# A hand-planned transformer kernel on one core: the first q stores move to SP's queue, the rows of maxima to ScalarE's, small loads and an all-reduce go ahead of the feed-forward loads

## The chip, the cores and the metric

One core of a Trainium2 chip. The metric is the device time of one execution in microseconds (us), the median of several runs. TensorE is called PE, VectorE DVE, ScalarE ACT, GpSimd POOL, SyncE SP. "SPq" and "ACTq" in rows of the profile are DMAs issued from SP's and ACT's sequencers.

## The reference, cut to what matters

Two layers over 8 batches of 256 tokens, 512 wide. Layer 0 is causal ALiBi attention with 32 heads of 16 and one shared key and value head, plus a top-2-of-4 LoRA mixture. Layer 1 is a 16x16 attention inside each token plus a gated feed-forward of 1792.

```python
xn = _layernorm(x)
x = x + attn0(xn, Wqkv, Wo) + lora_moe(xn, A, B, Wr)
xn = _layernorm(x)
gate, up = dequant(xn, gate_wq, gate_scale), dequant(xn, up_wq, up_scale)
x = x + attn1(xn, Wq, Wk, Wv) + dequant(silu(gate) * up, down_wq, down_scale)
```

## The kernel before, in words

The tokens are worked in 4 chunks of 512 (c = 0 to 3), each of 2 batches (i = 0 to 7). Matrix products run on fp16 pairs, high and low part, three products for one. For each batch the kernel computes q, k and v, the scores once to find row maxima (step max, L1154 on PE, L1537 on DVE), a transpose of the maxima (nmT), then the scores again with the maxima as two extra rows of q, exponentials (exp: L1176 and L1171 on PE, L998 and L999 on ACT, low halves L883 on POOL or L1549 on DVE), the product with v (pv, L1191), the output projection (L1218) and the feed-forward (gate and up L1266, down L1287).

q needs another layout than the one it is computed in. Each tile of 128 columns is stored to DRAM (q_parts) by `store_heads` (L693) in pieces of 64 bytes, 1024 pieces to a DMA, and read back as rows of the tile `qq` (gather_first L705, gather L708). For chunk 0 that is step store(b, m) on ACT's queue, two DMAs each, 16 in all. For later chunks it is step q(c, m) on SP's queue, four DMAs for each of 4 tiles. These later tiles share two buffers `qs`, so ACT's step q(c, m) waits until the tile two before it is in DRAM. The maxima go into `qq` by step nm(i), two DMAs on SP's queue (L770), and exp(i, 0, 0) on PE waits for them.

```python
n = c * NK + m
wait_full(act, "q", c, m)
if n - 2 >= NK:
    act.wait_ge(s_qd[(n - 2) % NK], 16 * 2 * NB * ((n - 2) // NK))
```

The feed-forward weights (12 loads of 448 KB, step ffn_load, L859 and L862) and nine small loads (step late, L852; late(2) alone is 1 MB) are issued from POOL, on the software DMA queue. ffn_load(0) waits for gather(1), because it overwrites the place of q's weights and of `q_first`. late(2) waits for nm(0).

The order of the steps on each engine comes from a list scheduler that runs when the file is loaded: each step has a cost (US), its predecessors with a gap (Plan.add), and a rank (RANK) that decides among steps that could start. The kernel then issues each engine's steps in that order, with semaphores. So numbers in US, in RANK and in the gaps set the order on every engine, and nothing else.

Of the kernel before, what the change touches and what calls it, by code (L numbers as in the profile page):

```python
# [109 lines left out]
RANK = {  # L110
    "PE": {"xT0": (-48.5, -1, 4), "tok": (-300.5, 0, 19, -10), "kT": (224, 0.5, -46, 146), "q0": (-50, 0.5, 13, -67),
        "norm": (-268, 3, -40, 81), "norm2": (-397.5, 0, 0, -21), "qa": (184.5, -1, 55, 284), "q": (-63, 0, 64, 3),
        "max": (-171, 0.5, -40, -10), "nmT": (-110, 2, -10, 84), "exp": (-13, 0, 0, -214), "pv": (49.5, -2, -14, -17),
        "attT": (-191, 2, 6, -16), "midT": (428.5, 0, -6, 10), "outa": (-90.5, 4, -4, -94), "out": (111.5, 3, 22, -55),
# [16 lines left out]
    "POOL": {"start": (338, 0.5, 34, 23), "ffn_load": (-280, 1, 13, 3), "ln0": (468.5, 1, -41, 144), "clear": (-81.5, 2, -1, -103),
        "turn": (176, 4, -29, 20), "norm": (-170, 1, -10, 39), "late": (244.5, 4, 0, 29), "norm2": (-191, 3, -46, 131),
        "lo": (520, -2, -13, -11), "setup1": (-258.5, 1, -53), "setup2": (491.5, 3, -40, 154), "exp": (-533, 4),
        "ln1": (-398, -2, -24, -97), "att4": (416, -2, -81, 153), "up": (-667.5, 0.5, -49, -52)},
    "SP": {"x_load": (361, 4, 3, 2), "consts": (395, -2, -26, 1), "wo": (438, 2, 247, -23), "gather_first": (-18, 3, -6, -235),
        "gather": (68, 2, -86, -160), "tables": (142, 1, -7, 41), "q": (952.5, 4, -60, 97), "nm": (211, 1, 0, 264),
        "x1_load": (-206.5, 2, -14), "down": (215.5, 2, 0, 129)},
}


# [1590 lines left out]
```

## Time and profile before

| | us |
|---|---|
| median of 3 runs | 625.62 (624.89 to 625.85) |
| the profiled execution | 625.02 |
| its span | 623.2 |
| PE busy | 570.7 (92%) |
| DVE, ACT, POOL busy | 461.3, 377.0, 351.7 |

The profiled execution's span leaves 1.8 us of its own time outside. Times of rows count from the start of the span. A row's bracket is the idle time of the engine before the row and what ended it.

### The profile page before, as it was taken

What the parts mean: (1) busy time and instruction counts of PE and PEld (TensorE: products, weight loads), DVE (VectorE), ACT (ScalarE), POOL (GpSimd) and SP (SyncE); (2) the same over time, 40 slices, a digit from 0 to 9 for tenths busy, and PEclk for the clock granted to TensorE, in tenths of its full rate; (3) what the DMA queues carried; (4) which work ended last, traced back from release to release, by engine and by line L of the source; (5) the groups of instructions that cost most, each with busy time, mean ns of one, the idle gap of its engine ahead of it and who ended that gap; (6) DMA issues with size and microseconds to landing.
All of it is one profiled execution on the core that took longest, in us unless ns stands there. A gap on an engine that the chain in (4) does not pass through costs nothing.

```text
span 623.2 us, 14286 instructions
## 1 busy us (share of the span) xinstructions
PE 570.7 (92%) x5590; PEld 421.3 (68%) x5590; DVE 461.3 (74%) x1034; ACT 377.0 (61%) x703; POOL 351.7 (56%) x364
## 2 busy tenths in 40 slices
PE   4579583699999999999999999999999999999997
PEld 4466451467885668776968587858685876785783
DVE  4769874899999874899697748996986569354642
ACT  3287095847875478675757485858684776651240
POOL 6231595724655667674837574848576677542140
PEclk9987895599999999999999999999999999999999
DMA  8767799905054146001610160016001000000000
GB/s 207 152 95 78 123 237 217 170 2 54 2 54 87 37 68 70 3 4 35 88 17 5 35 86 4 4 35 88 1 5 52 18 1 9 28 2 2 35 1 34
DMA packets 98942, 34.97 MB, mean 56 GB/s; under 512 B 75548, under 2 KB 90044, under 8 KB 98876
## 3 DMA queue, kind: packets, MB, share of 16 engines
q1 hardware_dynamic: 76044, 24.58, 22.7%
q0 software_dynamic: 2352, 7.18, 5.7%
q10 hardware_dynamic: 20480, 2.31, 2.6%
q8 instruction: 44, 0.72, 0.5%
q14 instruction: 22, 0.18, 0.1%
HBM read 30.19 MB, written 8.39 MB: 62 GB/s over the span
## 4 chain that ended last, share of the span: by engine, by line
PE 68%; DVE 13%; SPq 8%; ACT 4%; issue 3%; DMA 2%; POOL 2%; ACTq 1%; DVEq 0%
PE B_bank L1266 27%; PE B_bank L1287 14%; PE A_bank L1218 7%; SPq L693 5%; PE A_bank L1191 4%; DVE mx L1537 4%; PE A_bank L1120 3%; PE E_bank L1176 3%; PE B_bank L1154 3%; PE E_bank L1171 2%; PE B_bank L1254 1%; DMA qq<-nmp 1%; ACTq L693 1%; SPq L731 1%; SPq L717 1%
## 5 line engine op out<-in xcount | busy, mean ns | idle before, releaser
L883 POOL TENSOR_TENSOR probs<-e,probs 128x512 f16<-128x512 f32 x176 | 208.3, 1188 | 127.2 <-ACT probs L999 126.8
L1266 PE MATMUL B_bank<-xs,wgu 128*128 128x256 f16 x1792 | 204.3, 273 | 0.3 <-DVE hf L1649 0.3
L998 ACT ACTIVATE e<-E_bank,wn 128x512 f32<-128x512 f32 x192 | 133.7, 696 | 103.4 <-PE E_bank L1176 53.9
L1266 PEld LDWEIGHTS B_bank<-xs,wgu 128*128 128x128 f16 x1792 | 172.7, 98 | 21.6 <-DVE hf L1649 0.6
L999 ACT ACTIVATE probs<-E_bank,wn 128x512 f16<-128x512 f32 x192 | 134.0, 698 | 0.0
L1287 PE MATMUL B_bank<-wd,hbuf 128*128 128x512 f16 x448 | 99.9, 379 | 0.1
L897 POOL TENSOR_TENSOR hbuf<-hf,hbuf 128x512 f16<-128x512 f32 x56 | 65.8, 1176 | 56.2 <-ACT hbuf L1033 55.8
L1537 DVE TENSOR_REDUCE mx<-B_bank 128x2 f32<-128x384 f32 (+5 forms) x168 | 92.1, 603 | 4.5 <-PE B_bank L1154 4.4
L1639 DVE SCALAR_TENSOR_TENSOR hf<-ebuf,B_bank 128x512 f32<-128x512 f32 x56 | 38.3, 684 | 62.2 <-ACT ebuf L1043 61.9
L1287 PEld LDWEIGHTS B_bank<-wd,hbuf 128*128 128x128 f16 x448 | 43.2, 98 | 49.3 <-POOL hbuf L897 0.6
L1043 ACT ACTIVATE ebuf<-B_bank,sgx 128x256 f32<-128x256 f32 x112 | 47.5, 485 | 22.1 <-PE B_bank L1266 20.8
L1176 PE MATMUL E_bank<-qq,kk 128*128 128x256 f16 x256 | 47.8, 285 | 11.9 <-ACT probs L999 6.0
L1191 PEld LDWEIGHTS A_bank<-vv,probs 128*128 128x128 f16 x1536 | 47.8, 97 | 12.0 <-issue 8.4
L1191 PE MATMUL A_bank<-vv,probs 128*128 128x33 f16 x1536 | 49.0, 179 | 7.3 <-DVE probs L1549 7.2
L1649 DVE SCALAR_TENSOR_TENSOR hf<-B_bank,sux,hf 128x256 f32<-128x256 f32 x112 | 48.9, 478 | 4.9 <-PE B_bank L1266 3.8
L1154 PE MATMUL B_bank<-kk,qq 128*128 128x256 f16 (+7 forms) x512 | 47.7, 231 | 0.7
L1033 ACT ACTIVATE hbuf<-hf 128x512 f16<-128x512 f32 x56 | 35.5, 634 | 19.3 <-DVE hf L1649 19.1
L1218 PE MATMUL A_bank<-wo,attnT 128*128 128x512 f16 x192 | 46.2, 379 | 0.2 <-issue 0.2
L1154 PEld LDWEIGHTS B_bank<-kk,qq 128*128 128x128 f16 x512 | 33.3, 100 | 14.3 <-DVE mx L1537 4.0
L1176 PEld LDWEIGHTS E_bank<-qq,kk 128*128 128x128 f16 x256 | 23.4, 99 | 24.6 <-ACT probs L999 10.9
L1120 PE MATMUL A_bank<-xa,wq 128*128 128x512 f16 x144 | 34.7, 384 | 0.8 <-DVE xa L1369 0.8
L866 POOL TENSOR_SCALAR rs<-mv 128x1 f32<-128x1 f32 x32 | 10.0, 314 | 39.3 <-DVE mv L1406 39.2
(199 smaller groups left out, 696.3 us busy)
## 6 DMA issues: line engine op xcount, KB each, us to landing
qq<-q_parts SPq DMA_DIRECT2D x21, 256.0 KB
x<-in_x SPq DMA_DIRECT2D x20, 256.0 KB, 3.1
out_y<-x SPq DMA_DIRECT2D x16, 256.0 KB, 2.0
xa<-in_x SPq DMA_DIRECT2D x12, 256.0 KB, 5.1
q_parts<-qs SPq DMA_DIRECT2D x48, 64.0 KB, 2.9
wgu<-in_gate_w POOLq DMA_DIRECT2D x4, 448.0 KB, 9.1
wgu<-in_up_w POOLq DMA_DIRECT2D x4, 448.0 KB, 8.7
wd<-in_down_w POOLq DMA_DIRECT2D x4, 448.0 KB, 7.1
```

The costliest lines, as they stand in the source:

```text
L883: pool.tensor_tensor(probs[:, u % PSLOTS, 1, :], e32[:, w, :], probs[:, u % PSLOTS, 0, :], ALU.subtract).then_inc(s_lop, 1)
L897: pool.tensor_tensor(h_pair(u, 1, i), hf[:, n % 2, :], h_pair(u, 0, i), ALU.subtract).then_inc(s_hl, 1)
L998: act.activation(e32[:, w, :], psum("exp", i, g, w)[:, :], ACT.Exp, scale=wn[:, 7:8])
L999: act.activation(probs[:, u % PSLOTS, 0, :], psum("exp", i, g, w)[:, :], ACT.Exp, scale=wn[:, 7:8])\
L1120: mm = pe.matmul(psum("q", c, m)[:, :].rearrange("p (t n) -> p t n", t=NT), wq2[:, k, wpart, m * P:(m + 1) * P], xp[:, :, xpart, k, :], st ...
L1154: mm = pe.matmul(acc[:, g, :], tokens, keys.rearrange("p t k -> p (t k)")[:, 0:width], start=True, stop=True, skip_group_check=True)
L1176: mm = pe.matmul(acc[:, c0:c0 + blocks, :, :], kk[:, b, half, w, :], tokens[:, t0:t0 + blocks, :, :], start=True, stop=True, skip_group_ch ...
L1191: mm = pe.matmul(pvb[:, qt, j, :], probs[:, (3 * n + w) % PSLOTS, part, j * P:(j + 1) * P], vv[:, c % 2, 2 * b + kt, :], start=(kt == 0 an ...
L1218: mm = pe.matmul(psum("out", i, t)[:, :], tokens, wo2[:, k, wpart, :], start=(k == 0 and n == 0), stop=(k == NK and n == 1))
L1266: mm = pe.matmul(psum(name, u, i)[:, a * SEQ:(a + 1) * SEQ].rearrange("p (t n) -> p t n", t=NU), wgu[:, m, k, (2 * i + a) * P:(2 * i + a + ...
L1287: mm = pe.matmul(psum("down", u, t)[:, :], hbuf[:, u % 2, part, i, t * P:(t + 1) * P], wd[:, i, :], start=(i == 0 and part == 0), stop=(i ...
L1537: dve.tensor_reduce(mx[:, i % 2, g0:g0 + count], psum("max", i, n)[:, 0:count * width].rearrange("p (g k) -> p g k", g=count), AX.X, ALU.m ...
```

## The change

Four parts. (1) Step store(b, m) is issued by SP, not ACT. (2) Step nm(i) is issued by ACT, not SP, for all 8 batches. (3) late(2) to late(8) wait for gather(1), not for nm(0), and ffn_load(0) to (11) come behind late(8). (4) Costs, gaps and all ranks are new, which moves steps on every engine. Among them POOL's all-reduce of the scale maximum (setup1) comes before the loads, and in the plan takes 7.4 in place of 0.5.

```diff
-      "SP": {"wo": 1.4, "x_load": 2.4, "consts": 5.0, "tables": 5.8, "q": 0.5, "gather": 2.1, "gather_first": 1.4, "nm": 1.2, "x1_load": 0.5, "down": 0.5}}
+      "SP": {"store": 1.6, "wo": 1.4, "x_load": 2.4, "consts": 5.0, "tables": 5.8, "q": 0.5, "gather": 2.1, "gather_first": 1.4, "x1_load": 0.5, "down": 0.5}}
...
-    "PE": {"xT0": (-48.5, -1, 4), "tok": (-300.5, 0, 19, -10), "kT": (224, 0.5, -46, 146), "q0": (-50, 0.5, 13, -67),
+    "PE": {"xT0": (123.5, 0, 0, -50), "tok": (-422.5, -2, -40, 76), "kT": (-79, 1, -45), "q0": (-141, -2, 47, 24),
...
-    p.add("ACT", ("nmT", i), pe("nmT", i), *([sp("nm", i - 1)] if i else []))
+    p.add("ACT", ("nmT", i), pe("nmT", i), *([act("nm", i - 1, gap=2.5)] if i else []))
-    p.add("SP", ("nm", i), dve("nmT", i))
+    p.add("ACT", ("nm", i), dve("nmT", i))
...
-        p.add("ACT", ("store", b, m), dve("q0", b, m))
+        p.add("SP", ("store", b, m), dve("q0", b, m))
...
-        p.add("POOL", ("ffn_load", n), sp("gather", 1, gap=8.0), at=34.0 + 5.0 * n)
+        p.add("POOL", ("ffn_load", n), pool("late", 8), at=34.0 + 4.0 * n)
...
-                p.add("POOL", ("late", n), *([sp("nm", 0), pool("lo", NK)] if n > 1 else []), at=14.0)
+                p.add("POOL", ("late", n), *([sp("gather", 1, gap=6.0), pool("lo", NK)] if n > 1 else []), at=14.0)
...
+            def store(b, m):
+                wait_used(sp, "q0", b, m)
+                store_heads(sp, 0, b, m, q_first[:, b, m, :, :], s_q0[b][m])
...
                 if n == 2:
-                    pool.wait_ge(s_nmrow[0], 32)
+                    pool.wait_ge(s_gather[1], 16 * 3)
                     pool.wait_ge(s_wlo, NK + 1)
...
+            def nm(i):
+                b = i % 2
+                wait_used(act, "nmT", i)
+                for part in range(2):
+                    act.dma_start(qq[R_NM + part:R_NM + part + 1, b, :, :, :].rearrange("o c h t -> o (c h t)")
+                                 .rearrange("o (g n) -> o g n", n=P), nmp[:, part, :]).then_inc(s_nmrow[b], 16)
```

How the order changes at three places. The first is POOL's queue from the last low halves of the q weights on (wq, wtok, wo are low halves of weights, L859 and L856 feed-forward loads, L852 and L849 the small loads). Before:

```order
L830 TENSOR_TENSOR wtok<-ebuf,wtok 128x4x100
L866 TENSOR_SCALAR rs<-mv 128x1
L868 TENSOR_TENSOR rs<-rs,mhalf 128x1
L878 ISA
L878 ISA cmax<-cmax 128x1
L830 ISA
L830 TENSOR_TENSOR wo<-hbuf,wo 128x512 x4
L830 TENSOR_TENSOR wo<-hbuf,wo 64x512
L859 DMA wgu<-in_gate_w 128x1792
L859 DMA wgu<-in_up_w 128x1792
```

Changed, the same place:

```order
L827 TENSOR_TENSOR wtok<-ebuf,wtok 128x4x100
L849 DMA xs<-in_wq 128x4x512
L849 DMA ytmp<-in_bq 128x512
L849 DMA bias<-in_bk 128x16
L849 DMA bias<-in_bv 128x16
L849 DMA ebuf<-in_wk 128x4x16
L849 DMA ebuf<-in_wv 128x4x16
L849 DMA dsb<-in_down_s 128x512
L827 TENSOR_TENSOR wo<-hbuf,wo 128x512
L856 DMA wgu<-in_gate_w 128x1792
L856 DMA wgu<-in_up_w 128x1792
```

The all-reduce (L878) has left this place for one ahead of chunk 1's statistics, and the seven small loads stand where it stood. Nine feed-forward loads now stand ahead of POOL's first exp step, six before.

The second place is ACT's queue ahead of batch 0's exponentials (qs is step q(1, m), nmp is nmT(0)). Before:

```order
L972 ACTIVATE qs<-A_bank 128x512
L985 ACTIVATE gex<-gex 128x16
L972 ACTIVATE qs<-A_bank 128x512 x2
L1013 ACTIVATE nmp<-A_bank 64x128
L998 ACTIVATE e<-E_bank,wn 128x512
```

Changed:

```order
L965 ACTIVATE qs<-A_bank 128x512 x2
L1006 ACTIVATE nmp<-A_bank 64x128
L1012 DMA qq<-nmp 1x64x128 x2
L965 ACTIVATE qs<-A_bank 128x512
L991 ACTIVATE e<-E_bank,wn 128x512
```

nm(0) is new on this queue, and q(1, 3), which stood behind the fourth exp step before, is now ahead of the first.

The third place is SP's queue from the tables on (probs are tables, wd and qs the q tiles to store). Before:

```order
L748 DMA qq<-probs 3x8x1024 x4
L705 DMA qq<-q_parts 16x8x256 x12
L708 DMA qq<-q_parts 16x32x256 x3
L693 DMA q_parts<-qs 128x8x32 x8
L770 DMA qq<-nmp 1x64x128 x2
L693 DMA q_parts<-qs 128x8x32 x4
```

Changed:

```order
L748 DMA qq<-probs 3x8x1024 x4
L693 DMA q_parts<-wd 128x8x32 x8
L705 DMA qq<-q_parts 16x8x256 x6
L693 DMA q_parts<-wd 128x8x32 x2
L705 DMA qq<-q_parts 16x8x256 x6
L693 DMA q_parts<-wd 128x8x32 x6
L708 DMA qq<-q_parts 16x32x256 x3
L693 DMA q_parts<-qs 128x8x32 x12
L717 DMA xa<-in_x 128x512 x4
```

The 16 stores of chunk 0 are threaded between the gathers, and x_load(2) (L717) stands behind twelve stores of chunk 1, as before.

## Rows read from the trace of the kernel before

**Rows 1.** Windows: busy time of each engine in three stretches.
```profile
core 0: us, PE busy (x) PEld busy (x) DVE busy (x) ACT busy (x) POOL busy (x), PEclk, DMA share, GB/s
...
99.00:106.00 7.00, 0.30 (x2) 0.00 (x0) 3.34 (x9) 0.78 (x2) 2.43 (x4) 0.50 0.97 221
...
125.00:140.00 15.00, 14.38 (x156) 9.19 (x155) 14.14 (x31) 6.14 (x12) 4.19 (x6) 1.00 0.01 2
...
200.00:300.00 100.00, 98.53 (x986) 70.22 (x984) 81.90 (x180) 69.21 (x130) 65.23 (x65) 1.00 0.24 42
```

**Rows 2.** Timeline of ACT and its queue: start, us, what [idle before <-releaser].
```profile
26.27 5.59 ACTq L693 DMA_DIRECT2D q_parts<-wd  x2
31.90 0.60 ACT L955 ACTIVATE xa<-A_bank 128x512 f32<-128x512 f32 x1 [5.77 <-issue]
...
78.42 0.69 ACT L998 ACTIVATE e<-E_bank,wn 128x512 f32<-128x512 f32 x1 [11.54 <-PE E_bank L1176]
...
106.14 0.69 ACT L998 ACTIVATE e<-E_bank,wn 128x512 f32<-128x512 f32 x1 [6.36 <-DVE probs L1549]
...
119.44 0.67 ACT L998 ACTIVATE e<-E_bank,wn 128x512 f32<-128x512 f32 x1
```

**Rows 3.** Timeline of DVE (three rows), then of PE (one).
```profile
58.88 0.68 DVE L1459 SCALAR_TENSOR_TENSOR qs<-A_bank,qs 128x512 f16<-128x512 f32 x1
...
69.63 0.28 DVE L1543 SCALAR_TENSOR_TENSOR nmp<-A_bank,nmp 64x128 f16<-64x128 f32 x1
...
102.48 0.69 DVE L1405 BATCH_NORM_STATS2 st<-xa 128x6 f32<-128x512 f32 x1 [7.66 <-DMA xa<-in_x]
...
116.42 0.61 PE L1176 MATMUL E_bank<-qq,kk 128*128 128x256 f16 x2 [2.66 <-DMA qq<-nmp]
```

**Rows 4.** Timeline of SP's queue: start, us, what.
```profile
17.65 7.18 SPq L748 DMA_DIRECT2D qq<-probs  x4
33.13 6.61 SPq L705 DMA_DIRECT2D qq<-q_parts  x12
50.92 1.36 SPq L708 DMA_DIRECT2D qq<-q_parts  x3
...
71.38 23.66 SPq L693 DMA_DIRECT2D q_parts<-qs  x4
95.08 4.11 SPq L717 DMA_DIRECT2D xa<-in_x  x4
...
108.26 1.51 SPq L770 DMA_DIRECT2D qq<-nmp  x2
```

**Rows 5.** Timeline of POOL, 62 to 69 us.
```profile
62.81 5.61 POOL L830 TENSOR_TENSOR wo<-hbuf,wo 128x512 f16<-128x512 f32 x5 [7.00 <-issue]
68.37 0.74 POOL L859 DMA_DIRECT2D wgu<-in_gate_w  x1
```

**Rows 6.** DMA queues (packets, MB, share), 56:60, then 59:68 with 40 slices, then 78:84.
```profile
q1 hardware_dynamic: 465, 0.23, 66.9%
...
DMA  0000001878878878888820387877878888881000
...
q1 hardware_dynamic: 8320, 0.52, 55.5%
...
q0 software_dynamic: 388, 1.26, 104.0%
q1 hardware_dynamic: 388, 0.02, 10.1%
```

**Rows 7.** Tile q_parts on SP, 59:67, then 69:96 (durations in ns).
```profile
L693 SPq DMA_DIRECT2D q_parts<-qs x8: 359/584/597, 59.6 to 64.8; - x8
...
DMA to landing us min/median/max: 2.1/2.6/2.8
...
L693 SPq DMA_DIRECT2D q_parts<-qs x4: 605/3790/15346, 71.4 to 89.7; - x4
...
DMA to landing us min/median/max: 9.8/22.6/25.7
```

More of the change, by code:

```diff
@@ L131 @@
[L131 to L137, printed above, removed]
+    "PE": {"xT0": (123.5, 0, 0, -50), "tok": (-422.5, -2, -40, 76), "kT": (-79, 1, -45), "q0": (-141, -2, 47, 24),
+        "norm": (-183.5, 4, 71, 10), "norm2": (-274.5, 3, -33, -203), "qa": (279, -2, 17, 164), "q": (-269, 0.5, 4, -32),
+        "max": (-64.5, -2, -10, 7), "nmT": (-117.5, 2, -6, 256), "exp": (55.5, 0.5, -8, -60), "pv": (122.5, 2, 23, -121),
+        "attT": (-658.5, -1, 27, -14), "midT": (158, 1, 129, 20), "outa": (38.5, 1, 51, 15), "out": (142.5, 4, 0, -153),
[8 rows of a table added]
+        "mix": (213, -1, -5, -53), "mixb": (-144, 2, 3, 83), "norm": (-341.5, -1, -8), "scale": (-92, -1, -3, 6),
+        "scaled": (-284.5, 4, 20, 3), "tables": (332, -1, 10, -136), "hot": (791.5, 1, 11), "norm2": (-207.5, 2, 0, -83),
+        "scale2": (415.5, 0.5, 36, 80), "setup0": (566, 1, 114), "setup1": (121, 2, -1, -9), "setup3": (53, 3, 5, -9),
+        "xT0": (-690, 3, 13, 40), "q": (-141.5, 2, 2, 49), "max": (99, 0.5, -56, 34), "nmT": (-287, 4, -25, 86),
+        "exp": (-315, -2, -17, -31), "pv": (-227.5, 3, -78, -40), "attT": (-655, 0, -20), "out": (-20, 3, 31, -43),
+        "ln1": (197.5, 0, -114, -65), "xn1": (-250.5, 1, -1, -15), "xT1": (691.5, -1, 0, 6), "tok1": (-241.5, -2, 10, -13),
+        "att1": (-235.5, 1, 22, 17), "att2": (-643, 2, -109, -65), "att3": (227.5, 3, 20), "att4": (-237.5, -2, 3),
+        "gate": (-220.5, -1, 20, -233), "up": (-526.5, 0.5, 0, -16), "down": (176.5, 0, 0, -343)},
@@ new lines @@
+    "POOL": {"start": (96, 1), "ffn_load": (-532.5, 1, 19), "ln0": (289.5, -2, 51, -2), "clear": (94, 0, 21, 27),
+        "turn": (-287.5, -2, 78, 25), "norm": (-109, -2, 91, -24), "late": (515, -2, 7, 20), "norm2": (-519, 4, 17, 10),
+        "lo": (589.5, 1, 6, 51), "setup1": (625, 3, 71, 108), "setup2": (102.5, 0.5, -30, -13), "exp": (296.5, 1, 7, 26),
+        "ln1": (-188, 3, -44, 10), "att4": (-362, 1, 25, 17), "up": (678, 2, 89, 61)},
+    "SP": {"x_load": (179, 3, -78, 3), "consts": (131.5, 1, -9, -1), "wo": (330, 4, 15, -33), "store": (171, -2, -182, 22),
+        "gather_first": (-35, 3, -69, 25), "gather": (-273.5, -2, -10, 2), "tables": (-84, -1, 28, -37), "q": (362.5, 4, 5, -3),
+        "x1_load": (1191, 3, 26, -11), "down": (-142, 4, -20, -37)},
@@ L351, in query @@
         for m in range(NK):
-            p.add("SP", ("gather_first", m), ("ACT", ("store", 0, m), 4.5))
+            p.add("SP", ("gather_first", m), sp("store", 0, m, gap=4.5))
     for b in range(NB):
@@ L356, in query @@
             continue
-        stored = [sp("q", c, m) for m in range(NK)] if c else [("ACT", ("store", 1, m), 4.5) for m in range(NK)]
-        p.add("SP", ("gather", i), *stored, *([sp("gather_first", NK - 1, gap=0.0)] if i == 1 else [sp("nm", i - 1, gap=0.0)]), *([pe("exp", i - 2, NHG - 1, 2)] if c else []))
+        stored = [sp("q", c, m) for m in range(NK)] if c else [sp("store", 1, m, gap=4.5) for m in range(NK)]
+        p.add("SP", ("gather", i), *stored, *([sp("gather_first", NK - 1, gap=0.0)] if i == 1 else [act("nm", i - 1, gap=0.0)]), *([pe("exp", i - 2, NHG - 1, 2)] if c else []))
     p.add("DVE", ("mix", c), dve("tok", c, 1), *([pe("midT", 2 * c - 1)] if c else []))
@@ L423, in plan @@
             p.add("DVE", ("scaled",), dve("scale"))
-            p.add("DVE", ("tables",), sp("consts"))
+            p.add("DVE", ("tables",), sp("consts", gap=3.0))
             p.add("SP", ("tables",), dve("tables"))
@@ L439, in plan @@
                 p.add("POOL", ("lo", n), act("hi", n))
-            p.add("DVE", ("setup0",), pool("late", 1, gap=6.0))
-            p.add("DVE", ("setup1",), pool("late", 8, gap=8.0), dve("nmT", 0))
+            p.add("DVE", ("setup0",), pool("late", 1, gap=7.0))
+            p.add("DVE", ("setup1",), pool("late", 8, gap=14.0), dve("nmT", 0))
             p.add("POOL", ("setup1",), dve("setup0"))
@@ L1045, in gate_ @@
                 sig.then_inc(s_sig, 1)
-            run("ACT", {"start": start, "squares": squares, "squares2": squares2, "hi": hi, "nmT": nmT, "midT": turn_mid, "store": store, "xT0": xT0, "q0": q0, "q": q, "kT": kT, "mix": mix, "exp": exp, "attT": attT,
+            run("ACT", {"start": start, "squares": squares, "squares2": squares2, "hi": hi, "nmT": nmT, "nm": nm, "midT": turn_mid, "xT0": xT0, "q0": q0, "q": q, "kT": kT, "mix": mix, "exp": exp, "attT": attT,
                         "xT1": xT1, "att2": att2, "gate": gate_, "up": up})
```

36 lines of the change are left out of this document (7 added, 29 removed), and 16 rows, old and new, of tables (RANK, US).

## The prediction

> **What bounds the kernel now.** I read the windows first. From about 125 us to the end PE has no idle time worth naming: 14.38 us busy of 15 from 125 to 140, 98.53 of 100 from 200 to 300, at a granted clock of 1.00, its level of 2.4 GHz [rows 1]. Nothing that the change touches can shorten this part except by starting it earlier. What can move is the head. There I read the timeline of each engine and what ended its idle time.
>
> The head has four losses that belong to the places changed. ACT's queue is held for 5.59 us by two stores of chunk 0 and ACT sits idle for 5.77 us until 31.90, where PE waits for its copy [rows 2]. Batch 0's exponentials start on ACT at 78.42 and batch 1's at 119.44: 41.0 us [rows 2]. In that stretch ACT waits 6.36 us for DVE, which itself waits 7.66 us for chunk 2's x [rows 2, 3]; from 99 to 106 PE is busy for 0.30 us of 7 at a granted clock of 0.50, that is at 1.2 GHz [rows 1]. That x is late because its loads are issued only at 95.08, behind four q stores that hold SP's queue from 71.38 for 23.66 us [rows 4]. Last, PE waits 2.66 us for nm(1) at 116.42, whose DMAs were issued at 108.26 [rows 3, 4].
>
> Why four stores of 64 KB take 23.66 us is the key to this case. With no other traffic, eight such stores make 8320 packets, and the slices show each four done in 15 slices of 0.225 us, 3.4 us, some 1220 packets per us [rows 6]; each lands 2.1 to 2.8 us after issue [rows 7]. From 78 to 84 us, with feed-forward loads waiting on the software queue, both queues make exactly 388 packets: they take turns one for one, 64.7 per us each, and a packet of the software queue carries 3.2 KB [rows 6]. The same stores then land 9.8 to 25.7 us after issue [rows 7]. So a q tile, 4160 packets, costs 3.4 us alone and would cost 64 us beside weight loads without a pause.
>
> **The change, part by part.**
>
> *Stores of chunk 0 on SP.* ACT's 5.77 us are gone [rows 2]. ACT then is the chain through chunk 0: I place step q(1, 0) on DVE at 57, not 58.88 [rows 3], because most of the gain goes to SP. SP issues the tables until 24.83 [rows 4]. The third store was not accepted on ACT's queue before about 31 [rows 2]; I take the same for SP, whose ring also holds the tables (bounds: held not at all, 6 us earlier; held as long again, 6 later). From 31.3: five more stores 3.5, six gathers 3.3 (12 take 6.61), two stores 1.2, six gathers 3.3, six stores 3.5, landing 2.6, which gives gather(1) at 48.7 against 50.92 [rows 4, 7]. Its transfer was still busy for 0.669 of the stretch from 56 to 60, so it ended near 59 [rows 6]; 8 us after issue. Changed: 57.
>
> *Small loads ahead, weights behind them.* POOL waited 7.00 us in the all-reduce and then did five low halves until 68.37, the first weight load [rows 5]. The all-reduce moves to about 30 us. Queued behind it there are chunk 1's statistics, which DVE waits for; POOL is through by 37 to 42, before ACT has its weights done, so I cost it at 0 (if that cover fails, up to 7.0). POOL is then ready when gather(1) lands. Seven small loads at some 0.65 us (a weight load takes 0.74 [rows 5]) and one low half of 1.1: the first weight load issues near 62.7, 5.7 us earlier than before. Seven loads follow at once and two more within 10 us, since POOL's first exp step stands behind nine. Nine loads are 9 x 0.459 MB, at 1.26 MB in 6 us [rows 6] 19.7 us: without a pause from 64.3 (1.6 us after issue) to 84.0, say 85 with the slow first one.
>
> *What that train does to q.* Step q(1, 0) is stored from 57, q(1, 1) from about 65. In before both were in DRAM by 68, ahead of the first weight load. Now 8320 packets meet the loads. Before the train some 3000 to 4000 get through (1.6 us alone, then beside the small loads and in gaps), in it 20 us x 64.7 = 1300. Left: about 4000, 3.3 us after the train, and 1.5 for the landing. ACT's q(1, 3) waits for q(1, 1) in DRAM and now stands ahead of the first exponential; PE, DVE and POOL queue behind it. Exponentials start at 85 + 3.3 + 1.5 + 0.6 for q(1, 3) + 0.3 = **91**, 12.6 later than 78.42. nm(0)'s low half, at 69.63 before [rows 3], moves some 3 us ahead as mixb no longer stands before it; that too is swallowed by this wait.
>
> *nm on ACT.* Two issues, 1.51 us on SP [rows 4], now on ACT: for batch 1 that is +1.5 in the stretch. nm(1) no longer lies behind six x loads, so 2.66 goes [rows 3]. The Trainium skill, page "DMA: Bandwidth & Descriptors", section "Issuing engines are not separate DMA queues", says that issuing elsewhere saves only the sequencer's time; by that nm(1) would stay as late, and the sum would be 2.7 higher. The rows show nm only on SP's queue, so nothing here decides it yet. For the six later batches I take 0: PE is the bound there and ACT is busy 69 of 100 us [rows 1]; without that cover it is 1.5 each, 9.
>
> *x for chunk 2.* Still behind twelve stores, so issued near 94, landed by 100. DVE wants it some 20 us after the exponentials start, at 111. The 6.36 go.
>
> *Ranks and costs.* From 125 on the same products in another order: 0, between -1.5 (PE's idle of 200 to 300) and +1.5 (as much again) [rows 1].
>
> **The sum**, against the profiled execution's 625.0: start +12.6, stalls -6.4 and -2.7, nm +1.5, q(1, 3) and one copy already done -1.0. That is +4.0: **629.0**. The median before is 0.6 above the profiled execution, well inside what I can resolve, so I leave it.
>
> **The rivals.**
>
> *The train does not hold the stores.* If q(1, 1) lands 3 us after issue, nm(0), issued near 66.5 (69.63 less the 3 us above), lands 7 to 8 us later, as nm(1) did beside loads [rows 3, 4], and exponentials start at 74.5: -3.9 in place of +12.6, so 625.0 - 3.9 - 9.1 + 0.5 = 612.5. For it: every part of the change then helps, and both stalls go. Against it: 388 to 388 [rows 6]. It decides if the train starts after about 68 or has long pauses. One form of it is that the queues do not take turns by single small pieces: at nine or more pieces a turn, 4160 need 462 turns, 7 us, and the start is near 76, the end 614. The same page, section "Queues, rings and completion order", states such a rule, whole packets of about 9 to 17 descriptors. The trace's counts speak against it here. 0.25 for both forms together, 0.04 of it the latter.
>
> *The wait only cancels.* With gather(1) landed at 53 (SP never held), the train ends by 81 and exponentials start at 87: 625. Or two of the loads slip behind exp steps, -4. The place is the same as in the forecast, only shorter. 0.12.
>
> *Slower on another wait.* gather(2) waits for the last exp step of batch 0 and lands over 8 us later; if chunk 1's last stores or chunk 2's x still crowd the ring then, max(2, 0) is 4 to 8 us later still: 633 to 637. It decides if exponentials start after 95. 0.07.
>
> *The change does not do what it says*: SP held by the tables' DMAs as ACT was, so that chunk 0 gains nothing. Then gather(1) lands at 59 or later, all above shifts by 2: 631. This lies in the forecast's own range.
>
> **How the numbers follow.** The forecast, the train holding q(1, 1), has 0.56, with a range of its own of 625 to 633 (landing of gather(1) -3 to +2, exponentials' stretch plus or minus 2). Of it 0.05 is within 0.2%. By 0.2%, 1.25 us, about what a measurement here can tell: faster is 0.25 plus 0.04 from the cancelling case, 0.29; same 0.05 plus 0.08, 0.13; slower 0.51 plus 0.07, 0.58. The range takes in the better part of the fast rival and leaves out its lower half and the end of the slow one: 613 to 635.
>
> **What would show it.** Right: ACT has a gap of over 15 us between 62 and 91 in front of qs (L965), q stores issued from 57 to 66 land after more than 15 us, queue counts of both queues are equal from 66 to 84, x for chunk 2 is not waited for, and PE waits for nm(1) under 1 us. Wrong: exponentials (L991) start before 80, or the q(1, 1) stores land within 5 us. Wrong in size: the start is at 91 and the end is not 4 us later, because the stretch of 32 us up to batch 1 was mis-sized.

## The result, and the profile after

The changed kernel takes **633.8 us** in the median of 4 runs (631.33 to 635.14), the kernel before, run between them, 625.74 (624.89 to 626.0). The ratio is 1.0127, with a 95% interval of 1.0094 to 1.0159: 6 to 10 us slower. The profiled execution is the fastest of the four, 631.33 us with a span of 629.5; the one before took 625.0 with 623.2. The rows come from these profiled executions, so the sum is checked against 631.3 less 625.0, which is +6.3. For the 2.5 us by which the median lies higher there is no trace.

The timeline of ACT and its queue, which answers to [rows 2]:

```profile
56.76 0.60 ACT L965 ACTIVATE qs<-A_bank 128x512 f16<-128x512 f32 x1 [6.62 <-PE A_bank L1120]
...
85.86 0.60 ACT L965 ACTIVATE qs<-A_bank 128x512 f16<-128x512 f32 x1 [20.89 <-DMA q_parts<-qs]
...
88.33 1.54 ACTq L1012 DMA_DIRECT2D qq<-nmp  x2
...
91.99 0.60 ACT L965 ACTIVATE qs<-A_bank 128x512 f16<-128x512 f32 x1 [5.38 <-DMA q_parts<-qs]
...
93.06 0.69 ACT L991 ACTIVATE e<-E_bank,wn 128x512 f32<-128x512 f32 x1 [0.47 <-PE E_bank L1176]
...
125.69 0.70 ACT L991 ACTIVATE e<-E_bank,wn 128x512 f32<-128x512 f32 x1
```

ACT waits 20.89 us for q(1,0) in DRAM, 5.38 more for q(1,1), and only then starts the exponentials, at 93.06 instead of 78.42. From there to batch 1's first exponential it needs 32.6 us instead of 41.0. Batch 1 therefore starts 6.25 us late, and the whole kernel ends 6.3 us late. PE has a part in it too: its product for q(1,3) stands behind q(1,2):

```profile
87.23 4.18 PE L1120 MATMUL A_bank<-xa,wq 128*128 128x512 f16 x12 [18.71 <-DVE qs L1459]
```

Then POOL's timeline (answering to [rows 5]), one row of DVE (to [rows 3]), and SP's queue (to [rows 4]):

```profile
34.22 0.38 POOL L875 PARTITION_ALL_REDUCE cmax<-cmax  x1 [5.76 <-issue]
41.60 0.73 POOL L816 TENSOR_TENSOR wm<-wm,mhalf 128x2 f32<-128x2 f32 x1 [7.00 <-issue]
...
58.00 0.94 POOL L849 DMA_DIRECT2D xs<-in_wq  x1 [8.54 <-DMA qq<-q_parts]
...
64.15 0.72 POOL L856 DMA_DIRECT2D wgu<-in_gate_w  x1
```

```profile
43.29 0.55 DVE L1417 TENSOR_SCALAR xa<-x,mv,rs 128x512 f32<-128x512 f32 x1 [3.15 <-POOL rs L865]
```

```profile
48.84 1.38 SPq L708 DMA_DIRECT2D qq<-q_parts  x3
58.84 33.20 SPq L693 DMA_DIRECT2D q_parts<-qs  x12
92.08 2.12 SPq L717 DMA_DIRECT2D xa<-in_x  x4
...
98.86 5.82 SPq L774 DMA_DIRECT2D x<-in_x  x6
122.99 1.39 SPq L708 DMA_DIRECT2D qq<-q_parts  x3
```

Twelve q stores hold SP's queue for 33.20 us. The DMA queues say why. The first two rows are 60 to 68 us, the next two 78 to 84 (as in [rows 6]), the last is 88 to 91, when no load is left:

```profile
q0 software_dynamic: 611, 1.83, 78.7%
q1 hardware_dynamic: 3120, 0.20, 26.8%
...
q0 software_dynamic: 398, 1.25, 105.2%
q1 hardware_dynamic: 397, 0.03, 9.3%
...
q1 hardware_dynamic: 2714, 0.17, 59.6%
```

Beside the train, the weight loads that follow each other without a pause, it is 398 packets against 397, 66 per us for each queue; alone SP's queue makes 905 per us, and for part of these 3 us it has nothing to do. Equal counts alone would fit nine for nine as well as one for one. The records of the single packets, which the trace holds and no view prints, decide it: from 78 to 84 us each of the 397 small packets is followed within 8 ns by the start of one of the loads', and no more than two packets of one queue start in a row. The loads that I called small are these, in the list of DMA issues:

```profile
xs<-in_wq POOLq DMA_DIRECT2D x1, 1024.0 KB, 6.0
...
ytmp<-in_bq POOLq DMA_DIRECT2D x1, 256.0 KB, 5.7
dsb<-in_down_s POOLq DMA_DIRECT2D x1, 256.0 KB, 5.3
```

With the four smaller ones they make 1616 KB, as much as 3.6 weight loads of 448 KB. They hold q(1,0)'s stores more than one for one: the first store is issued at 58.84, and from 58 to 63 us the software queue makes 228 packets and SP's queue 59. One instruction sums up nearly every run of this case, batch 2's first maxima on PE (L1154). They start at 125.62 before and at 133.11 now, 7.5 us later, and the span ends 497.6 and 496.4 us after them. So 1.2 us more are lost between batch 1's first exponential and these maxima, and won back behind them; the cause of neither was looked for.

### The profile page after: what moved, and what is told of

Its sections match the earlier page's. It is cut to its first block, busy times and chain, and to the rows that moved or that the text cites. A ratio compares the mean times of both kernels' runs of the same rounds, so it can differ in the third digit from the quotient of the medians.

```text
span 629.5 us, 14288 instructions
## 1 busy us (share of the span) xinstructions
PE 572.2 (91%) x5590; PEld 418.2 (66%) x5590; DVE 449.4 (71%) x1034; ACT 376.9 (60%) x703; POOL 353.3 (56%) x364
## 4 chain that ended last, share of the span: by engine, by line
PE 71%; DVE 12%; SPq 5%; ACT 4%; issue 4%; POOL 2%; DMA 1%; ACTq 0%; POOLq 0%
PE B_bank L1266 28%; PE B_bank L1287 15%; PE A_bank L1218 7%; PE A_bank L1191 5%; DVE mx L1537 4%; PE E_bank L1176 4%; PE B_bank L1154 3%; PE A_bank L1120 3%; SPq L693 3%; PE E_bank L1171 2%; PE B_bank L1254 1%; ACT probs L992 1%; PE B_bank L1241 1%; SPq L731 1%; PE A_bank L1202 1%
## 5 line engine op out<-in xcount | busy, mean ns | idle before, releaser
L992 ACT ACTIVATE probs<-E_bank,wn 128x512 f16<-128x512 f32 x192 | 133.1, 693 | 0.0
L1154 PE MATMUL B_bank<-kk,qq 128*128 128x256 f16 (+7 forms) x512 | 49.0, 233 | 5.0 <-DVE mx L1537 3.6
L1154 PEld LDWEIGHTS B_bank<-kk,qq 128*128 128x128 f16 x512 | 33.2, 101 | 20.0 <-DVE mx L1537 8.5
L1120 PEld LDWEIGHTS A_bank<-xa,wq 128*128 128x128 f16 x144 | 14.0, 100 | 34.9 <-DVE qs L1459 19.0
```

The lines of the kernel that those rows point to most:

```text
L992: act.activation(probs[:, u % PSLOTS, 0, :], psum("exp", i, g, w)[:, :], ACT.Exp, scale=wn[:, 7:8])\
L1120: mm = pe.matmul(psum("q", c, m)[:, :].rearrange("p (t n) -> p t n", t=NT), wq2[:, k, wpart, m * P:(m + 1) * P], xp[:, :, xpart, k, :], st ...
L1154: mm = pe.matmul(acc[:, g, :], tokens, keys.rearrange("p t k -> p (t k)")[:, 0:width], start=True, stop=True, skip_group_check=True)
```

## The experiments

All were compared with the kernel before on the same chip; its medians were 625.6 to 626.3. In the table, "exp(0)" is the first exponential on ACT, "exp(1)" batch 1's first, "gather(2)" its issue on SP, "max(2)" batch 2's first maxima on PE, all in the profiled execution, and "rest" is the span less max(2).

| run | exp(0) | exp(1) | gather(2) | max(2) | rest | median us | ratio to before, 95% |
|---|---|---|---|---|---|---|---|
| before | 78.4 | 119.4 | 113.1 | 125.6 | 497.6 | | |
| changed | 93.1 | 125.7 | 123.0 | 133.1 | 496.4 | 633.80 | 1.0094 to 1.0159 |
| e1_hold | 77.5 | 113.0 | 110.8 | 122.9 | 497.3 | 621.96 | 0.9921 to 0.9966 |
| e2_late_nm0 | 76.7 | 114.5 | 117.5 | 128.3 | 499.0 | 629.08 | 1.0037 to 1.0080 |
| e3_four_qs | 78.0 | 113.1 | 110.4 | 120.8 | 495.8 | 618.49 | 0.9870 to 0.9940 |
| e4_nm_sp | 98.8 | 132.4 | 129.7 | 139.9 | 495.9 | 635.57 | 1.0091 to 1.0185 |
| e5_hold_all | 80.2 | 120.2 | 117.7 | 131.7 | 507.5 | 640.87 | 1.0199 to 1.0299 |
| e7_allred | 72.5 | 113.4 | 110.7 | 120.8 | 496.0 | 619.67 | 0.9852 to 0.9922 |
| e8_part1 | 73.0 | 120.2 | 109.7 | 126.3 | 498.3 | 621.67 | 0.9898 to 0.9951 |
| e9_best | 71.7 | 112.3 | 109.6 | 119.2 | 496.5 | 618.43 | 0.9834 to 0.9902 |
| e10_pool_order | 79.7 | 116.3 | 112.7 | 126.7 | 497.2 | 625.44 | 0.9964 to 1.0004 |
| e11_pool_4qs | 76.9 | 111.2 | 108.4 | 122.6 | 496.9 | 623.24 | 0.9928 to 0.9984 |
| e12_part2 | 80.6 | 120.9 | 116.5 | 128.8 | 498.5 | 626.56 | 0.9989 to 1.0031 |
| e13_spread | 71.9 | 112.3 | 108.9 | 120.5 | 495.9 | 618.29 | 0.9867 to 0.9930 |

**Hold the loads.** A later wait in ffn_load, in place of the one for gather(1), which the small loads ahead of it keep. The orders stay as they are:

```diff
                 if n == 0:
-                    pool.wait_ge(s_gather[1], 16 * 3)
+                    pool.wait_ge(s_qd[0], 64)
+                    pool.wait_ge(s_qd[1], 64)
```

> The changed kernel with one wait more: the first feed-forward load also waits until q(1,0) and q(1,1) are in DRAM. Orders are untouched. Theory (the train of loads holds the 64-byte stores one for one, and ACT's q(1,2) and q(1,3) wait for them): q(1,1)'s stores land within 5 us instead of 20, the gaps of 18.5 us on DVE and 20.9 us on ACT ahead of q(1,2) and q(1,3) go, and ACT's first exp starts at 75 to 77 instead of 93. POOL's first exp step stands behind nine loads that now begin near 72, so it comes near 85 and takes part of the gain back: 617 to 624 us. Rival (the stores are slow by themselves, or ACT waits for something else): the gap stays over 15 us, the first exp stays at 90 or later, 633 to 640 us.

Timeline of ACT, POOL and SP's queue, of this run:

```profile
69.05 0.60 ACT L966 ACTIVATE qs<-A_bank 128x512 f16<-128x512 f32 x1 [4.31 <-DMA q_parts<-qs]
...
77.45 0.69 ACT L992 ACTIVATE e<-E_bank,wn 128x512 f32<-128x512 f32 x1 [1.08 <-PE E_bank L1177]
```

```profile
73.30 0.57 POOL L857 DMA_DIRECT2D wgu<-in_gate_w  x1 [9.04 <-DMA q_parts<-qs]
```

```profile
75.76 6.09 SPq L717 DMA_DIRECT2D xa<-in_x  x4
82.30 25.31 SPq L693 DMA_DIRECT2D q_parts<-qs  x4
```

A kernel that does the same work and waits more is 12 us faster. ACT's 20.89 us at q(1,2) become 4.31. The train is still there, from 73.30, but now it holds q(1,3), for which nobody waits before gather(2). POOL's part came as expected in kind, smaller in size: ACT's fourth exponential waits 2.81 us for it.

**Take ACT's wait away instead.** Two buffers more for chunk 1 (q_buf gives m = 2, 3 a place in hidden activations that are unused then; the waits of chunk 2 follow, and the planner's orders come out the same):

```diff
-                if n - 2 >= NK:
+                if c == 2 and m < 2:
+                    act.wait_ge(s_qd[m], 16 * 2 * NB)
+                if c > 1:
                     act.wait_ge(s_qd[(n - 2) % NK], 16 * 2 * NB * ((n - 2) // NK))
-                act.activation(qs[:, m % 2, 0, :], psum("q", c, m)[:, :], ...
+                act.activation(q_buf(c, m)[:, 0, :], psum("q", c, m)[:, :], ...
```

> The changed kernel with two more buffers for chunk 1's q tiles (in a part of the hidden activations' memory that is unused then), so that ACT's q(1,2) and q(1,3) wait for no store. The loads and their order are untouched, so the stores stay slow. Theory (what costs is ACT's wait, not the slow stores as such): q(1,1)'s stores still land after 15 us or more, but the first exp starts at 74 to 77; x for chunk 2 is still issued after 88 on SP's full queue, so ln0(2,0) waits some 6 us: 614 to 622 us. Rival (the exponentials' operands, gather or nm(0), are held by the loads as well): first exp after 85, 626 us or more.

SP's queue, then ACT and DVE:

```profile
59.18 37.92 SPq L699 DMA_DIRECT2D q_parts<-qs  x8
97.14 2.64 SPq L699 DMA_DIRECT2D q_parts<-hbuf  x4
99.83 2.13 SPq L723 DMA_DIRECT2D xa<-in_x  x4
```

```profile
78.02 0.69 ACT L999 ACTIVATE e<-E_bank,wn 128x512 f32<-128x512 f32 x1 [3.90 <-PE E_bank L1184]
```

```profile
103.10 0.69 DVE L1413 BATCH_NORM_STATS2 st<-xa 128x6 f32<-128x512 f32 x1 [2.80 <-DMA xa<-in_x]
```

The stores are even slower, 37.92 us for eight, and the kernel is 15 us faster than the changed one. So the slow stores cost little by themselves (2.80 us of DVE's time here, for the x behind them): what costs is ACT's wait for them, ahead of the exponentials. These two runs, by different means, settle the forecast's mechanism.

**The third part undone** (the small loads wait for nm(0) again; the planner puts the weight loads behind them):

```diff
-                p.add("POOL", ("late", n), *([sp("gather", 1, gap=6.0), pool("lo", NK)] if n > 1 else []), at=14.0)
+                p.add("POOL", ("late", n), *([act("nm", 0, gap=2.5), pool("lo", NK)] if n > 1 else []), at=14.0)
...
-                    pool.wait_ge(s_gather[1], 16 * 3)
+                    pool.wait_ge(s_nmrow[0], 32)
```

> The changed kernel with the third part undone: the seven small loads wait for nm(0) again, and the weight loads stand behind them, spread over exp steps. Theory: no weight load is in flight while q(1,0) to q(1,3) are stored, so ACT's first exp starts at 74 to 77, x for chunk 2 is issued by 82; 611 to 618 us. Rival (the loss is in the new ranks or in nm on ACT's queue): within 3 us of the changed kernel's 633.

The start is as expected, 76.7, the end is not: 629.1. The same train ran later: six x loads then held SP's queue from 87.73 for 26.74 us, and gather(2) was issued at 117.49, 4.4 us later than before. A train costs wherever something small stands behind it. But this is no clean test of the third part: the changed edge made the planner move steps on every engine, some 150 of PE's 755 and some 100 of ACT's 434.

**Weight loads behind q(1,3), replanned** (the first load waits for all four tiles in DRAM, and the planner has that as an edge):

```diff
-                    pool.wait_ge(s_gather[1], 16 * 3)
+                    for m in range(NK):
+                        pool.wait_ge(s_qd[m], 16 * 2 * NB)
...
-        p.add("POOL", ("ffn_load", n), pool("late", 8), at=34.0 + 4.0 * n)
+        p.add("POOL", ("ffn_load", n), pool("late", 8), sp("q", 1, NK - 1, gap=9.0), at=80.0 + 3.0 * n)
```

> The changed kernel with the weight loads behind q(1,3)'s stores in DRAM and spread one by one between POOL's exp steps; the planner replans with that edge. Theory: q stores of chunk 1 land in 3 to 5 us each, first exp at 74 to 77, x for chunk 2 issued by 83 and landed before it is wanted, gather(2) as early as in the kernel before: 609 to 616 us, below both kernels. Rival (loads that are put off collide with x, gather(2) or the first gate): the start is at 75 but batch 2's maxima or the first gate wait over 5 us: 618 to 626 us.

This expectation failed, on both sides. exp(0) came at 80.2, and 10 us went after max(2): PE is busy for 93.89 us of 200 to 300, where the changed kernel has 99.51. The edge made the planner move steps on every engine, some 130 of PE's 755, and these orders seem to be worse; that was not tested by itself. The run says nothing on the train. From here on I edited orders by hand, except for the rows of maxima on SP's queue, where the planner moved next to nothing else.

**The all-reduce moved back** behind the last low half ahead of POOL's wait for gather(1), and no other step moved:

```diff
 ORDER = plan()
+_pool = ORDER["POOL"]
+_step = _pool.pop([s for _, s in _pool].index(("setup1",)))
+_pool.insert([s for _, s in _pool].index(("late", 2)), _step)
```

> The changed kernel with one step moved in POOL's order: the all-reduce stands behind the last low half before POOL's wait for gather(1), instead of ahead of chunk 1's statistics. Theory: chunk 1's normalized x waits no 3.15 us for POOL, q(1,0) is on DVE at 54.5 to 56 instead of 58.13; the train of weight loads starts at the same time (64 us), so 3000 more small packets are through before it and q(1,1) is in DRAM 2 to 4 us after the train's end as before or even ahead of its second half: first exp at 85 to 92, 627 to 633 us. Rival (the all-reduce was covered): q(1,0) at 58, first exp at 93, 633 to 635 us.

```profile
53.24 0.38 POOL L878 PARTITION_ALL_REDUCE cmax<-cmax  x1 [6.22 <-issue]
58.12 0.94 POOL L852 DMA_DIRECT2D xs<-in_wq  x1 [4.50 <-DMA qq<-q_parts]
...
72.50 1.15 POOL L830 TENSOR_TENSOR wo<-hbuf,wo 128x512 f16<-128x512 f32 x1 [9.52 <-issue]
73.60 0.74 POOL L859 DMA_DIRECT2D wgu<-in_gate_w  x1
```

q(1,0) was on DVE at 55.70, as expected, but exp(0) came at 72.5, far ahead of what I gave it, and the gain of 14 us is twice the largest I had. The reason stands in these rows: the all-reduce holds POOL's next arithmetic instruction, not its DMA issues. The seven loads went out at once, but the low half came 9.52 us after them, and the weight loads behind it at 73.60 instead of 64.15, by which time q(1,0) and q(1,1) were in DRAM. So this run tests two things at once, and the greater part is again the train's start.

**Rows of maxima of batches 1 to 7 on SP's queue**, in the changed kernel:

```diff
-    p.add("ACT", ("nm", i), dve("nmT", i))
+    p.add("SP" if i else "ACT", ("nm", i), dve("nmT", i))
```

> The changed kernel with the rows of maxima of batches 1 to 7 on SP's queue again (batch 0's stay on ACT's). Theory: on SP's queue nm(1) stands behind the six x loads of the feed-forward part, so its DMAs land 6 to 8 us after issue instead of 2.6 to 3.5, PE waits for it 1 to 4 us at its first exponentials of batch 1, and the two issues of 1.5 us leave ACT; net +1 to +3: 634 to 637 us. Rival (issuing elsewhere saves only the sequencer's time; the rings share the engines): nm(1) lands as early as on ACT's queue, no wait on PE, -1.5 us of issue time: 630 to 634 us.

```profile
72.14 0.60 ACT L977 ACTIVATE qs<-A_bank 128x512 f16<-128x512 f32 x1 [6.91 <-DMA q_parts<-qs]
...
98.29 0.60 ACT L977 ACTIVATE qs<-A_bank 128x512 f16<-128x512 f32 x1 [25.39 <-DMA q_parts<-qs]
```

Its time, 635.6, fits the theory, but the reason given for it is wrong: no PE waits for nm(1), which landed 3.2 to 3.5 us after issue, on an SP queue whose last issue had ended 4.5 us before. What the rows show is the train again: here q(1,0) got through and q(1,1) did not, so the waits of 20.89 and 5.38 became 6.91 and 25.39, and exp(0) 98.8. Which tile is caught is decided by a few us. It may be why the changed kernel's runs spread over 3.8 us; that was not tested.

**The first part alone**, on the kernel before, with the stores merged into SP's order as the changed kernel has them:

```diff
+ORDER["ACT"] = [(t, s) for t, s in ORDER["ACT"] if s[0] != "store"]
...
+_sp[_s:_s + 4] = [(_sp[_s][0], s) for s in [("store", 0, m) for m in range(NK)] + [("gather_first", 0), ("gather_first", 1), ("store", 1, 0),
+                  ("gather_first", 2), ("gather_first", 3), ("store", 1, 1), ("store", 1, 2), ("store", 1, 3)]]
...
```

> The kernel before with the first part of the change alone: chunk 0's q stores on SP's queue, merged by hand into its order as the changed kernel has them; nothing else moves. Theory: ACT's 5.8 us idle go, q(1,0) is on DVE 2 to 4 us earlier; the weight loads still start behind the all-reduce and five low halves, near 66 to 68, when q(1,1) is in DRAM, so no train stands ahead of the first exp, which comes at 74 to 77; x of chunk 2 is as late as before: 621 to 625 us. Rival (chunk 0's gain never reaches the exponentials because gather(1), now behind stores on SP, is as late as before or later): 625 to 628 us.

It is faster than before, by 0.5 to 1.0%. Its profiled execution was the slowest of its seven, 626.4 us, so its rows show a bad case: exp(0) at 73.0, then DVE waits longer than before for chunk 2's x, and PE longer for nm(1).

```profile
99.08 0.69 DVE L1409 BATCH_NORM_STATS2 st<-xa 128x6 f32<-128x512 f32 x1 [9.97 <-DMA xa<-in_x]
```

```profile
117.18 0.61 PE L1180 MATMUL E_bank<-qq,kk 128*128 128x256 f16 x2 [6.81 <-DMA qq<-nmp]
```

This run also shows that an early first weight load is not enough to make the loss. Here it goes out at 64.04, in the changed kernel at 64.15. But q(1,1) is on DVE at 56.84 instead of 67.30, so its stores are through before the train, and in the order of the kernel before q(1,3) stands behind the first exponentials. By this comparison the new places of q(1,1) and q(1,3) belong to the cause; they were not tested alone.

**The second part alone**, on the kernel before (nm behind nmT on ACT, for batch 0 at once, for the others with two steps between):

```diff
+ORDER["SP"] = [(t, s) for t, s in ORDER["SP"] if s[0] != "nm"]
+for _i in range(2 * NCH):
+    _at = [s for _, s in ORDER["ACT"]].index(("nmT", _i)) + (1 if _i == 0 else 3)
+    ORDER["ACT"].insert(_at, (0.0, ("nm", _i)))
...
```

> The kernel before with the second part of the change alone: the rows of maxima of all batches are issued on ACT's queue, placed by hand behind nmT in its order; the other orders are untouched. Theory: nm(1) is issued near 98 instead of 108.26, lands by 105 and PE no longer waits 2.66 us for it; but ACT's order behind it still waits for chunk 2's x, whose stall (DVE 7.66 us) is upstream of the same point, so 621 to 626 us. Rival (batch 1's start is set by chunk 2's x alone and the issues cost ACT time in every batch): 625 to 630 us.

No change that can be measured, between the two theories. PE's wait for nm(1) is gone, but chunk 2's x still comes late (DVE waits 7.16 us), and nm(1) was issued at 107.39, not 98, since ACT itself stood behind that x. The landing of nm(1), in the view of tile nmp: first this run, on ACT's queue while stores and x loads fill SP's, then before, on SP's queue behind them.

```profile
L1016 ACTq DMA_DIRECT2D qq<-nmp x2: 475/548/622, 107.4 to 107.9; - x2
...
DMA to landing us min/median/max: 2.7/2.8/2.9
```

```profile
L770 SPq DMA_DIRECT2D qq<-nmp x2: 470/736/1001, 108.3 to 108.8; - x2
...
DMA to landing us min/median/max: 7.1/7.3/7.6
```

The queue is not all that differs: from 107 to 110.5 us here no weight load flies, and before, from 108 to 116, 238 packets of them do.

**A version that beats both.** On the changed kernel three of the edits above together: the all-reduce's place, the two buffers, the held loads:

```diff
+_pool.insert([s for _, s in _pool].index(("late", 2)), _step)
...
+            if c == 1 and m > 1:
+                return flat[:, (m - 2) * 2 * CHUNK:(m - 1) * 2 * CHUNK].rearrange("p (a n) -> p a n", a=2)
...
+                    pool.wait_ge(s_qd[0], 64)
+                    pool.wait_ge(s_qd[1], 64)
```

> Three edits on the changed kernel at once: the all-reduce behind the low halves, two more buffers for chunk 1's q, and the first weight load held until q(1,0) and q(1,1) are in DRAM. Theory: q(1,0) on DVE near 55, nm(0) lands in 3 us, first exp at 71 to 75, exponentials of batch 1 on ACT at 106 to 110; q(1,3)'s stores are slow beside the train and may hold SP's queue until 105, so gather(2) is the next wait: 609 to 616 us. Rival (gather(2) and the slow q(1,3) stores set batch 2 whatever the start): batch 2's maxima no earlier than 120, 616 to 620 us.

618.43, some 15 us below the changed kernel and 8 below before. The rival was nearer: exp(0) is at 71.7, but ACT then waits 8.1 us for POOL, whose exponential steps stand behind five low halves and nine loads, and max(2) is at 119.2. Over a single edit the three together gain nothing that can be measured: with the two buffers alone it was 618.49, with the all-reduce's move alone 619.67, and the intervals overlap. In all three runs gather(2) goes out only at 109.6 to 110.7.

**POOL's order alone**, on the changed kernel: all-reduce, low halves of wo, the seven loads, then exponential steps with one or two weight loads behind each pair:

```diff
+_rest[_at:_at] = [("setup1",)] + [s for s in _moved if s[0] == "lo"] + [s for s in _moved if s[0] == "late"]
+_loads = [s for s in _moved if s[0] == "ffn_load"]
+for _g, _n in enumerate((1, 1, 2, 2, 2, 2, 1, 1)):
+    _at = _rest.index(("exp", 0, _g, 1)) + 1
+    _rest[_at:_at] = _loads[:_n]
```

> The changed kernel with POOL's order alone edited: the all-reduce and the five low halves of wo stand behind wtok's low half, then the seven small loads, then exp steps, and the twelve weight loads one or two behind each pair of exp steps. No wait is added and no buffer. Theory: the loads start only after the first exp step, when q(1,0) and q(1,1) are in DRAM, and leave pauses, so no store waits for a train; q(1,0) on DVE at 55 to 56, first exp on ACT at 72 to 76, exponentials of batch 1 at 105 to 110, gather(2) issued at 103 to 109: 608 to 616 us. Rival (the gain ends at the next transfer: q(1,3)'s stores or x beside the spread loads hold SP's queue until 110 whatever the start, as in the run with q(1,1) waited for): 617 to 622 us.

```profile
79.21 0.60 ACT L977 ACTIVATE qs<-A_bank 128x512 f16<-128x512 f32 x1 [10.64 <-DMA q_parts<-qs]
```

```profile
66.55 0.94 POOL L861 DMA_DIRECT2D xs<-in_wq  x1
...
83.29 0.56 POOL L868 DMA_DIRECT2D wgu<-in_gate_w  x1
```

Neither theory had this. No weight load is issued before 83.29, and yet ACT, ahead of q(1,3), waits 10.64 us for q(1,1). What flies beside its stores, issued from 67.74, are the seven loads issued from 66.55, with wq1's 1 MB. They are a train too, and a worse one: from 68 to 72 us their queue makes 295 packets and SP's queue 5. And the weight loads, spread thin, still fly when gather(2) is issued (409 packets from 112 to 126 us, none from 123 to 133 in the changed kernel), and it takes 14.0 us to max(2) instead of 10.1.

The same with q_buf's two buffers:

```diff
-                act.activation(qs[:, m % 2, 0, :], psum("q", c, m)[:, :], ...
+                act.activation(q_buf(c, m)[:, 0, :], psum("q", c, m)[:, :], ...
```

> The same POOL order with the two more buffers for chunk 1's q. Theory: without the train ACT's q(1,2) waits for q(1,0) in DRAM only 2 to 6 us, and what the buffers save there is taken by nm(0)'s chain, which is then the later one: within 2 us of the run with POOL's order alone. Rival (ACT's wait is still on the path): 3 to 6 us faster than it.

With two buffers more, 2.2 us less in the median, on the edge between the theories; exp(0) 2.8 earlier. The intervals of the two overlap a little, so this stays a tendency.

**e9 with POOL's work spread**: three weight loads and one low half ahead of the first exponential step, the rest behind the steps of heads 0 to 6 (so many loads, so many low halves):

```diff
+_pool[_at:_at] = _loads[:3]
+_loads = _loads[3:]
+for _g, (_n, _l) in enumerate(((2, 0), (2, 0), (2, 1), (1, 0), (1, 1), (1, 1), (0, 1))):
+    _at = _pool.index(("exp", 0, _g, 1)) + 1
+    _pool[_at:_at] = _loads[:_n] + _lows[:_l]
```

> The run with three edits (618.43 us), with POOL's order alone edited further: three weight loads ahead of POOL's first exp step instead of nine, one low half instead of five, the other loads and low halves behind the exp steps of heads 0 to 6. Theory: ACT's first exp stays at 71 to 73, ACT no longer waits 8.1 us for POOL at its fourth, and no load is in flight when gather(2) is issued at 102 to 106, so batch 2's maxima start at 112 to 116 and the end comes 496 to 498 us after them, as in every run so far: 610 to 615 us with what lies around the span. Rival (POOL is too full in the stretch, 33 us of work in 30, or q(1,3)'s stores beside the spread loads still hold gather(2)): maxima no earlier than 118, 616 to 621 us.

618.29, the same as e9. ACT's wait for POOL at its fourth exponential fell from 8.1 to 0.9 us, and then another took its place: 5.19 us for DVE at 100.45. It is the odd one of the section at the end. SP's queue, held 28.45 us by q(1,3)'s stores until 102.9, came free for gather(2) only at 108.86 as well.

## Why the prediction was right, and where it was off

*Direction and mechanism*: slower, by a later start of the exponentials that the stalls removed later do not pay back. The size was off: by the medians the loss is 8.1 us, twice the 4.0 forecast, and 6.3 in the profiled executions. The range of 613 to 635 took in both directions, so that the time fell into it says little. Point by point:

- *Chunk 0.* q(1,0) on DVE at 57: 58.13. Here a cover failed that I had costed at 0. The all-reduce held POOL until 41.60 and chunk 1's x waited 3.15 us for it, so 0.75 us of ACT's 5.77 arrived. With the all-reduce moved back q(1,0) was at 55.70, and with the first part alone, which keeps the old orders, at 53.26. The bound for it, "up to 7.0", stood in the text; I chose the wrong end.
- *gather(1)* issued at 48.7 against 48.84, landed at 57 against 57.9 (POOL goes on at 58.00).
- *First weight load* at 62.7: 64.15.
- *The train.* Some 3000 to 4000 of 8320 packets ahead of it, 64.7 per us beside it: 3120 from 60 to 68, and 66 per us. Its end at 85: the counts stay nearly equal up to 87 (1104 and 1126 from 70 to 87), and the last packet of its nine weight loads starts at 87.63. **This is the term that was mis-sized**, "a train from 64.3 to 84, say 85". I took the loads ahead of it for small without looking at their bytes, and they are 1.6 MB. Of the 1.83 MB of the software queue from 60 to 68 they are all but 0.2, and they use the queue until 66.8. The weights' packets run from 66.6 to 87.6, 21.1 us for my 19.7.
- *Exponentials at 91*: 93.06. The path to it was only in part the one forecast. I had ACT stop at q(1,3), for q(1,1), stored from about 65 (it was from 68.01). ACT stopped 20.89 us at q(1,2), for q(1,0), and q(1,1) added 5.38. My own counts should have told me: with 3000 to 4000 packets ahead of the train, q(1,0) with its 4160 is not through either. Even with q(1,1) in DRAM earlier little would have been won: behind q(1,2), PE's product for q(1,3) ended at 91.41, and nm(0), issued at 88.33, landed by 92.4, while q(1,1) landed at 91.9. That these three ends fall within 1 us is luck; the forecast had one of them.
- *Stalls.* x for chunk 2 issued near 94 and not waited for: 92.08, no wait. nm(1) not waited for: so it was. Stretch: the terms of the sum give 32.4, for which the text says 32; 32.6.
- *nm on ACT*, 1.5 us: two issues of 1.12 us together at 109.68.
- *From 125 on, 0*: 1.2 more up to max(2) and 1.2 less behind it, so the 0 came out as two terms that cancel.

The sum of +4.0 thus misses 2.1 at the start and 0.2 in the stretch: 631.3 for 629.0.

Of the rivals, "the train does not hold the stores" is out. With it goes the form by the Trainium skill's rule ("DMA: Bandwidth & Descriptors", section "Queues, rings and completion order": an engine drains a packet of some 9 to 17 descriptors from a queue before it turns to the next); the counts of 398 and 397, of loads against 64-byte pieces, and the order of their starts say one for one. The forecast had taken the equal counts alone as proof, which they are not. Its price was too low as well: it gave 612.5 with exponentials at 74.5, and e7 with exponentials at 72.5 has 618.6 in its profiled run, since ACT then waits 7.61 us for POOL, which stands behind low halves and loads.

On nm(1), the same page's section "Issuing engines are not separate DMA queues" says that another issuing engine saves only the issue itself. No run tests that alone. On ACT's queue nm(0) and nm(1) landed 2.6 to 4.2 us after issue where few or no loads of the software queue flew (nm(1) in the changed kernel and in e12, nm(0) in e7 and e5) and 5.6 to 7.3 us where they filled it (nm(1) in e7 and e1, nm(0) in e12). SP's queue shows the same two levels: 3.2 to 3.5 us in e4, and 6.4 to 7.2 for nm(0) in the kernel before, which had no x load ahead of it. So the weight loads in flight explain most of it (nm(1) in e5 does not fit, with 3.2 to 3.3 us beside loads), and the page is not contradicted. That nm(1) is no longer waited for was forecast rightly, but the reason given, the x loads ahead of it, is not shown.

Left open: which of the new ranks cost what. Part 1 alone is 4 to 5 us faster, part 2 alone nothing, all four 8 slower. Part 3 undone, with the orders that the planner then wrote, brings back 4.7 of it. The parts do not add up; that each decides who meets the train is my reading of it. The new ranks, in the old kernel and without the other parts, were not run.

## What to carry to other kernels

In this case a store of many small pieces beside loads of large pieces went at one piece per large one, and at its start at fewer. So look up, before moving a load forward, which small transfers will be in flight then and which engine waits for them; give those a buffer, or hold the load. Count the bytes of every load that is called small. When a whole plan hangs on one late event (here batch 2's maxima), follow that event through each experiment, and edit one step of the order by hand rather than plan anew.

## What the runs showed of the hardware

**An all-reduce over partitions holds POOL twice.** POOL is idle 5.76 us ahead of it and 7.00 behind it, for an operation of 0.38 on 128x1. In e7 it is 6.22 and 9.52, and the 9.52 come behind seven DMA issues that went through between. So the next arithmetic instruction waits, and the issues do not. The Trainium skill, "GPSIMD Engine Reference", section "Instruction dispatch", has some 6 us for the first call of a freshly loaded function; the rows ahead agree with it in size, and it has nothing of the same again behind.

**A DVE instruction can wait inside itself for POOL.** The scaling of down_s, 128x512, takes 0.49 us in e9 and 5.83 in e13. First DVE in e9, then DVE and POOL in e13:

```profile
99.56 0.49 DVE L1540 TENSOR_SCALAR dsb<-dsb,cmax 128x512 f32<-128x512 f32 x1
```

```profile
93.99 5.83 DVE L1551 TENSOR_SCALAR dsb<-dsb,cmax 128x512 f32<-128x512 f32 x1
```

```profile
94.45 1.17 POOL L847 TENSOR_TENSOR wo<-hbuf,wo 128x512 f16<-128x512 f32 x1
95.57 2.25 POOL L901 TENSOR_TENSOR probs<-e,probs 128x512 f16<-128x512 f32 x2
97.77 0.57 POOL L880 DMA_DIRECT2D wd<-in_down_w  x1
98.36 1.16 POOL L847 TENSOR_TENSOR wo<-hbuf,wo 128x512 f16<-128x512 f32 x1
```

POOL works without a gap from 91.66, and DVE's instruction ends at 99.82, 0.3 us after POOL's last one, at 99.52. In e9 it began in a gap of POOL's, of 0.27 us. The Trainium skill, "SBUF — State Buffer", section "SBUF: two separate sides", names a pair of ports that these two engines share, locked by one for a whole instruction. It agrees in kind, but a wait for one instruction of POOL's would be some 1.2 us here, and the row shows one through several. That may have taken from e13 what its order had gained. It was seen once at this length (1.42 us in e2 is the next longest) and not tested by itself.
